# Matmuls without a consumer in one attention pair, and a changed order of dealt work in another

## The reference, cut to what matters

```python
xn = _layernorm(x)                       # x: (4, 4096, 1024)
x = x + _L0_attn_ref(xn, Wq, Wk, Wv) + _L0_ffn_ref(xn, w_gate, w_in, w_out)
# attention: Q, K, V = xn @ W.T, taken as 16 heads by a plain reshape
scores = einsum('hbqd,hbkd->hbqk', Q, K); atten = softmax(scores)
y = einsum('hbqk,hbkd->hbqd', atten, V).reshape(b, s, -1) + xn
attn = (y - mean(y)) / sqrt(var(y) + EPS)        # mean, var over a whole batch
# ffn: 8 experts, no activation in between, the top 2 by gate
logits = xt @ w_gate.T
y += gates[:, e:e + 1] * ((xt @ w_in[e].T) @ w_out[e].T)   # for each e
```

## Time and profile before

| | us |
|---|---|
| three runs | 5494.86, 5491.11, 5884.72 |
| median | 5494.86 |
| the profiled execution | 5494.86 |
| its span on the slowest core (core 2) | 5493.1 |
| spans of the eight cores | 5479.9 to 5493.1 |

### The profile page before, as it was taken

The page is one execution under the profiler, slowest core; times in us unless marked ns, Lnnn a source line. Parts: engine busy times, 40 slices in busy tenths (PEclk is TensorE's granted clock), DMA queues, the critical chain, the costliest instruction groups (busy, mean ns, idle before and its releaser), DMA issues.

```text
span 5493.1 us, 63320 instructions; the slowest of 8 cores (5479.9 to 5493.1 us)
## 1 busy us (share of the span) xinstructions
PE 4632.5 (84%) x19844; PEld 1784.1 (32%) x19844; DVE 1394.0 (25%) x3704; ACT 2379.8 (43%) x2275; POOL 146.5 (3%) x290
## 2 busy tenths in 40 slices
PE   3788888888888975888888888888839999999994
PEld 2333333333332113333333333332214444444441
DVE  2312211112121015121221212111044334444345
ACT  1466666666666541666666666665610000000000
POOL 1000000000000000000000000000000000000000
PEclk8799999999998556999999998986869999999997
DMA  4100000000000001000000000003025765557733
GB/s 66 20 1 5 5 1 5 1 5 5 1 5 4 0 4 28 4 5 1 5 5 1 5 1 5 5 1 62 1 32 91 123 104 89 90 88 121 123 66 88
DMA packets 86065, 173.97 MB, mean 32 GB/s; under 512 B 4864, under 2 KB 4864, under 8 KB 85760
## 3 DMA queue, kind: packets, MB, share of 16 engines
q0 software_dynamic: 83456, 161.54, 18.5%
q1 hardware_dynamic: 2304, 8.39, 0.4%
HBM read 323.06 MB, written 8.39 MB: 60 GB/s over the span
## 4 chain that ended last, share of the span: by engine, by line
PE 68%; ACT 14%; DMA 5%; DVE 5%; issue 5%; DVEq 2%; POOL 0%; ACTq 0%; POOLq 0%
PE P_S L483 17%; PE P_OT L389 16%; ACT AR L319 12%; PE P_S L549 12%; PE P_A L363 5%; PE P_B L363 5%; PE P_OT L567 4%; DMA AR<-woutT 4%; PE P_B L567 2%; PE P_A L567 2%; DMA xstg<-xb 1%; DVEq L693 1%; DVE gsc L694 1%; ACT AR L329 1%; PE P_B L372 1%
## 5 line engine op out<-in xcount | busy, mean ns | idle before, releaser
L319 ACT ACTIVATE AR<-P_S,consts 128x1024 bf16<-128x1024 f32 x2048 | 2251.4, 1113 | 1251.7 <-PE P_S L483 1246.2
L389 PE MATMUL P_OT<-AR 128*65 128x512 bf16 x4096 | 1338.6, 410 | 213.2 <-ACT AR L319 211.2
L483 PE MATMUL P_S<-AR 64*128 64x512 bf16 x4096 | 1363.9, 420 | 4.2 <-DVE xnTb L655 1.6
L549 PE MATMUL P_S<-AR 128*128 128x512 bf16 x4032 | 881.7, 381 | 75.0 <-DVE AR L809 57.0
L389 PEld LDWEIGHTS P_OT<-AR 128*65 128x65 bf16 x4096 | 345.1, 114 | 984.2 <-issue 966.7
L549 PEld LDWEIGHTS P_S<-AR 128*128 128x128 bf16 x4032 | 395.6, 98 | 559.4 <-issue 91.4
L483 PEld LDWEIGHTS P_S<-AR 64*128 64x128 bf16 x4096 | 243.0, 97 | 925.0 <-issue 918.8
L811 DVE TENSOR_TENSOR AR<-P_S,AR 128x512 bf16<-128x512 f32 x380 | 262.9, 692 | 417.0 <-PE P_S L549 417.0
L583 DVE CAST AR<-P_A 64x256 bf16<-64x256 f32 x256 | 106.5, 416 | 981.6 <-PE P_A L363 981.6
L583 DVE CAST AR<-P_B 64x256 bf16<-64x256 f32 x256 | 106.4, 416 | 973.3 <-PE P_B L363 973.3
L363 PE MATMUL P_A<-xnTb,AR 128*65 128x256 bf16 x2048 | 316.2, 305 | 1.5 <-DVE xnTb L655 1.5
(11 more groups left out here) (107 smaller groups left out, 1623.6 us busy)
## 6 DMA issues: line engine op xcount, KB each, us to landing
AR<-winN POOLq DMA_DIRECT2D x64, 1024.0 KB, 15.1
AR<-woutT POOLq DMA_DIRECT2D x64, 1024.0 KB, 24.2
xstg<-xb POOLq DMA_DIRECT2D x80, 256.0 KB, 4.4
out<-AR SPq DMA_DIRECT2D x16, 512.0 KB, 2.9
AR<-wqT POOLq DMA_DIRECT2D x2, 1024.0 KB, 14.2
AR<-wkT POOLq DMA_DIRECT2D x2, 1024.0 KB, 25.7
AR<-wvT POOLq DMA_DIRECT2D x2, 1024.0 KB, 36.9
identsb<-idin POOLq DMA_DIRECT2D x1, 32.0 KB, 2.1
```

The lines of the kernel that those rows point to most:

```text
L319: inst = ac.activation(AR[:, R_PT + sl * 1024: R_PT + (sl + 1) * 1024], stb[:, 0:1024], AF.Exp, bias=consts[:, 0:1])
L389: last = pe.matmul(pOT[0:65, hq * 512:(hq + 1) * 512], lhs, rhs, start=(k == 0), stop=(k == 31))
L483: last = pe.matmul(stb[0:128, hq * 512:(hq + 1) * 512], lhs, rhs, start=True, stop=True)
L549: last = pe.matmul(BK[bk][:, 0:512], lhs, rhs, start=(kt == 0), stop=(kt == 7))
```

## The change

It makes two edits. In pair 7, a new function `pe_keepalive` issues 8 matmuls of 128x128 by 128x256 at steps 1, 4, 10, 13, 21 and 25 of each block, 24 groups in all. They read `xnTb` and the V weights in place and write bank A or B in turn; nothing reads what they write, and the next user of the bank waits on TensorE's own count. In pair 15, the list `DL15` puts one `glog` item more ahead of the first `mmq` item, and shifts the rest by it.

```diff
-DL15 = (_GL[0:5] + [_MM[0], _GL[5], _GL[6], _MM[1], _GL[7], _GL[8],
...
-                    _MM[4], _GL[13], _GL[14], _MM[5], _GL[15]] + _MM[6:8])
+DL15 = (_GL[0:6] + [_MM[0], _GL[6], _GL[7], _MM[1], _GL[8], _GL[9],
...
+                    _MM[4], _GL[14], _GL[15]] + _MM[5:8])
@@ in _ab_schedule
+                elif pj == 7:
+                    for i in _dl15_qc(qc):
+                        seq.append(("dum", i))
@@ in emit_pe
+        def pe_keepalive(i):
+            bk = BANKOF[("dum", i)]
+            bacq(pe, bk)
+            last = None
+            for kt in range(8):
+                lhs = xnTb[:, kt * 2048 + (i % 8) * 256:
+                           kt * 2048 + (i % 8) * 256 + 128]
+                rhs = AR[:, R_WQKV + 16384 + kt * 1024 + (i % 4) * 256:
+                         R_WQKV + 16384 + kt * 1024 + (i % 4) * 256 + 256]
+                last = pe.matmul(BK[bk][:, 0:256], lhs, rhs,
+                                 start=(kt == 0), stop=(kt == 7))
+            inc(last, "sPE", ("dum", i))
+            brel(bk, ("dum", i))
@@ in the loop over steps
-                        elif (pj == 15
+                        elif (pj in (7, 15)
                               and k in (1, 4, 7, 10, 13, 17, 21, 25, 29)):
                             gs = 9 * qc + dealt
                             dealt += 1
                             if gs % 3 != 2:
-                                pe_deal15(_DEAL_GS.index(gs))
+                                if pj == 15:
+                                    pe_deal15(_DEAL_GS.index(gs))
+                                else:
+                                    pe_keepalive(_DEAL_GS.index(gs))
```

More of the change, by code:

```diff
@@ L70 @@
        ("mmq", 1, 1, 0), ("mmq", 1, 1, 1)]
-DL15 = (_GL[0:5] + [_MM[0], _GL[5], _GL[6], _MM[1], _GL[7], _GL[8],
-                    _MM[2], _GL[9], _GL[10], _MM[3], _GL[11], _GL[12],
-                    _MM[4], _GL[13], _GL[14], _MM[5], _GL[15]] + _MM[6:8])
+DL15 = (_GL[0:6] + [_MM[0], _GL[6], _GL[7], _MM[1], _GL[8], _GL[9],
+                    _MM[2], _GL[10], _GL[11], _MM[3], _GL[12], _GL[13],
+                    _MM[4], _GL[14], _GL[15]] + _MM[5:8])
 DEALT_MM = {(0, 0, 0), (0, 0, 1), (0, 1, 0), (0, 1, 1),
```

## The result

The changed kernel takes 5421.32 us (median of 8 runs, 5414.68 to 5740.44), the kernel before, run beside it, 5495.27 us. The ratio is 0.9863, with a 95% interval of 0.9848 to 0.9877, by which the time is 5420 us. The profiled execution took 5418.73 us, with a span of 5416.7 us on core 3. The forecast was 5411 us, in a range of 5400 to 5431.

A forecast was written before the change was run, and what follows sets the result against it. The prediction took TensorE as the bound, at 1.2 GHz in pair 7. Pair 7's -67.7 us and pair 15's +2.3 and -18.6 us sum to -84.0 us, from 5494.9 to 5411 us; range 5400 to 5431.

The forecast's parts named there:

- What bounds pair 7: Pair 7, with no dealt work: TensorE at 1.2 GHz is the bound, 69.66 us a block at 0.50.
- The rise at the step-1 group: Pair 7: the clock rises behind that group about 10.5 us into each block, one rise and one fall a block.
- -67.7 us: Pair 7 with 24 groups: 52.75 us a block, 211.0 us for the pair against 278.65.
- a rise at step 4: Pair 7: the clock rises only there in every block, costing 3 cold steps, 8 us in all: 5419 us.
- The first rival: Pair 7's clock rises late or falls again mid-block: eight cold steps a block, 22 us, 5433 us; chance 0.12.
- the likeliest one: The forecast case for the whole kernel, 5411 us; chance 0.75.
- It stays up between steps 13 and 21: Pair 7: the clock holds through the longest stretch without a group, as it held 34.1 us in pair 15.
- The rival of a second fall: Pair 7: the clock falls again between steps 13 and 21; priced with a late rise at 22 us, chance 0.12.
- The price of a group: Pair 7: a group costs 0.69 us net at close steps, 0.5 us at steps farther apart.
- +2.3 and -18.6: Pair 15's new order, in us: block 0 slower by the first, blocks 1 to 3 faster by the second.
- Elsewhere nothing: Second phase 0, gates and experts: same code at an earlier time; the experts have nothing to win.
- The rule that spoke against the change: Idle gaps throttle TensorE, sustained activity releases it; if groups don't raise pair 7's clock, 5520 us, chance 0.05.

## Why the prediction was right, point by point

*What bounds pair 7.* Right, and tested: with short matmuls in the same places the pair stays at 0.50 and 283.03 us, with solid ones it goes to 0.87 and 218.20. TensorE at 1.2 GHz was the bound.

*The rise at the step-1 group.* Right in blocks 0 and 2, wrong in block 1 on every core and in block 3 on two. This is the term that was mis-sized: "-67.7 us", from four equal blocks of 52.75 us, came out as -60.5 on core 3. Blocks 0 and 2 took 52.68 and 52.96 us; each late block took 3.5 us more. A late block 3 costs the second phase 0 another 2.5 us, which no term had. The rival had priced a rise at step 4 at three cold steps, 2 us a block; the rise came 8.7 us late, which is more than four. The first rival named the cause, "a phase drift between block and clock could do this in one or two blocks", and gave it 0.12 as a case of its own; it is part of the likeliest one. I took ordinary blocks as proof, which rise behind such a group every time. But there the rise always comes at nearly the same place, 10.2 to 10.9 us into all 54 such blocks of core 2 in the kernel before (without block 0 of pair 8, which holds the second phase 0); with other block lengths it need not, and dropping three groups changed the length. The kernel with one narrow group a block shows the miss by itself. What sets the moments of change the traces do not tell, beyond that they don't start with a block.

*It stays up between steps 13 and 21.* Right: 40.9 us at 1.00 with no group at all. The rival of a second fall did not occur in any block.

*The price of a group.* 0.5 us, measured at equal rise over five groups, where I took 0.69 for the close steps and 0.5 for the others. Weight loads of 128 columns cost nothing that can be seen: the step-4 group took 1767.69 - 1766.81 = 0.88 us in the changed kernel, by its timeline, against 0.90 in the earlier trace rows.

```profile
1766.81 1.05 PE L442 MATMUL P_B<-AR,xnTb 128*128 128x256 bf16 x8
1767.69 0.59 PE L392 MATMUL P_OT<-AR 128*65 128x512 bf16 x2
```

*Pair 15.* Right: +2.3 and -18.6 foretold, -16.3 in sum; measured -16.0, by block 70.66, 53.22, 52.06 and 55.68 us for 70.8 and "52, 52 and 55". The item that moved out of block 0 cost its 10 us at 2.4 GHz, the items that moved to step 1 brought the rise forward by 15.8, 20.2 and 15.9 us, 17 on the mean, as foretold.

*Elsewhere nothing.* Nearly right. The prediction named "a change of more than some 3 us in the second phase 0 or the experts" as proof of a wrong step. Behind pair 15 there are -3.8 us, but they lie within the spread of the cores and decide nothing; the +2.5 us in the second phase 0 are under the bound and yet an effect of the change, on the two cores with the late block 3.

*The rule that spoke against the change.* The trace shows the level down for whole blocks with gaps of 0.12 us between matmuls, and up for 40.9 us in the same pair. The Trainium skill (TensorE: Matmul & The Clock Gate) puts the fall down to idle gaps ("HAM oscillation") and the rise to activity ("What's actually happening"). The first half agrees in kind and not in size: with filled ends the level no longer fell at an ordinary block's end, but the example in the Trainium skill has waits of 3 to 5 us, where TensorE's longest single wait at the block end that was read, at 1695.26 in the kernel before, is 1.33 us, and the level fell in waits of 1.19 us too. The second half doesn't hold here as it stands: 278 us of nearly unbroken matmuls at 1.2 GHz did not raise the level, eight of one kind in a row did.

*The sum.* 5411 foretold, 5418.73 in the profiled execution; 7.2 of the 7.7 us between them are pair 7, nearly all of it the two late blocks. That the rest fits to 0.5 us is in part luck, since the cores differ by more than that behind pair 15. The prediction held 2% for about the least that a measurement of this kernel can tell from no change; the interval of 0.9848 to 0.9877 tells 1.4% from none with ease.

## What to carry to other kernels

Where two stretches of one loop differ in time and the one with less work is slower, look at the granted clock before anything else, by windows of one level, and read from the timeline what the engine did just before it rose and fell. A level that is kept by itself but must be won again after each pause is cheapest to win with one solid group right behind the pause, a wide one, since of the narrow ones some were missed, and cheaper still not to lose: matmuls in waits that exist anyway took another 2 us off each of the ordinary blocks. Check every such gain on all cores, since a rise that is nearly missed shows as the same code at two speeds on two cores, and the slowest core sets the time.

## What was not expected of the hardware

The level has a memory. In pair 7 the same steps of scores and V matmuls, with nothing dealt in, ran for 278 us at 0.50 in the kernel before, at 1.00 for 40.9 us behind one wide group, and at 1.00 for 191.48 us on core 2 of the kernel with filled block ends, although TensorE is busy for a smaller share of the time at the higher level (34.45 of 40.90 us, against 256.86 of 278.65). Which of the two it is goes by the level that the block has once its first wait is past. And less than a tenth of a microsecond decides: block 3 of pair 7 in the changed kernel rose 9.2 us in on core 0 (51.87 us) and 19.4 us in on core 3 (56.16 us), where the fall before lay 2.38 and 2.34 us into the block.
